# Runs selected tile by tile, halved adds and a mask made by ScalarE in a two-layer graph kernel

## The reference

```python
h = relu(layernorm(x))
W = einsum('rb,bio->rio', w_comp, weight)             # 16 types from 8 bases
x = x + segment_sum((h @ W[r])[etype, src], dst) + h_bias
h = relu(layernorm(x))
g = leaky(h @ enc_w + enc_b)                           # slope 0.1
for l in range(2):
    agg = segment_sum(g[src], dst) / max(degree, 1)
    g = leaky(agg @ lin_l_w[l] + lin_l_b[l] + g @ lin_r_w[l])
x = x + g
```

## Time and profile before

| | us |
|---|---|
| median of 3 runs | 3403.03 (3397.12 to 3404.61) |
| the profiled execution | 3396.55, its span 3394.8 |
| busy over the span | PE 2463.2 (73%), DVE 2900.7 (85%), ACT 1885.4 (56%), POOL 2461.0 (72%) |
| granted TensorE clock, mean | 0.905 |

### The profile page before, as it was taken

How to read it: one execution, slowest core, us unless ns; L and a number is a source line. 1 busy time by engine, 2 the same in 40 slices (tenths; PEclk the granted TensorE clock), 3 DMA queues, 4 the chain that set the end, 5 groups by cost and what they waited for, 6 DMA issues and landing times. The chain is left out here.

```text
span 3394.8 us, 49738 instructions
## 1 busy us (share of the span) xinstructions
PE 2463.2 (73%) x13942; PEld 1823.4 (54%) x13942; DVE 2900.7 (85%) x8116; ACT 1885.4 (56%) x4895; POOL 2461.0 (72%) x2412
## 2 busy tenths in 40 slices
PE   2999999999999588888888888657777746663000
PEld 2555555555555366666666666557777735553000
DVE  4899888888888599999999999689999978776567
ACT  1566666666666498888888888635555521110000
POOL 4477777777777477777777777577777757778871
PEclk9999999999999799999999999979999978776555
DMA  9989888887222599999999999479999989999999
GB/s 244 371 325 283 260 235 257 239 258 227 77 82 73 185 282 283 286 284 283 287 284 283 285 285 282 125 254 340 341 333 346 312 314 416 416 416 404 399 407 357
DMA packets 642447, 969.06 MB, mean 285 GB/s; under 512 B 70661, under 2 KB 412295, under 8 KB 630370
## 3 DMA queue, kind: packets, MB, share of 16 engines
q1 hardware_dynamic: 532598, 717.70, 62.9%
q0 software_dynamic: 85376, 194.22, 17.8%
q10 hardware_dynamic: 24198, 53.96, 4.7%
HBM read 509.25 MB, written 464.73 MB: 287 GB/s over the span
## 5 line engine op out<-in xcount | busy, mean ns | idle before, releaser
L972 PE MATMUL y_ps_rel<-w_basis,ht_rel 128*128 128x512 f32 x1568 | 754.3, 605 | 4.0 <-DVE two_rel L831 4.0
L709 POOL DMA_INDIRECT agg<-rows_rel,put_c x392 | 408.0, 1041 | 160.9 <-issue 96.1
L1251 ACT ACTIVATE h_node<-base_node,shift_node,rstd_node 128x128 f32<-128x128 f32 x1176 | 500.3, 483 | 1.6 <-DVE shift_node L1331 1.6
L368 POOL DMA_INDIRECT gat_rel<-in_x_dram,src_c x392 | 406.8, 1038 | 125.1 <-issue 109.9
L1111 POOL DMA_INDIRECT base_and_means<-rows_node,odd_c x392 | 388.1, 990 | 145.9 <-issue 118.0
L1102 POOL DMA_INDIRECT term_node<-agg,src_c x392 | 394.1, 1005 | 132.7 <-issue 119.6
L1792 POOL DMA_INDIRECT gat_l<-base_and_means,src_c x392 | 393.5, 1004 | 119.7 <-issue 119.4
L831 DVE SCALAR_TENSOR_TENSOR two_rel<-y_ps_rel,coef,two_rel 128x128 f32<-128x128 f32 x1568 | 438.4, 343 | 0.0
L972 PEld LDWEIGHTS y_ps_rel<-w_basis,ht_rel 128*128 128x128 f32 x1568 | 273.9, 195 | 199.2 <-issue 138.0
L984 PEld LDWEIGHTS sum_ps_rel<-same_rel,two_rel 128*128 128x128 f32 x1568 | 238.5, 192 | 191.0 <-issue 188.2
L912 ACT ACTIVATE part_rel<-y_ps_rel,coef 128x128 f32<-128x128 f32 x784 | 242.4, 361 | 159.2 <-PE y_ps_rel L972 158.7
(11 more groups left out here) (216 smaller groups left out, 6408.7 us busy)
## 6 DMA issues: line engine op xcount, KB each, us to landing
pairs_l<-base_and_means SPq DMA_DIRECT2D x112, 512.0 KB
base_and_means<-zero_row SPq DMA_DIRECT2D x49, 1024.0 KB
means<-zero_row SPq DMA_DIRECT2D x49, 1024.0 KB, 10.9
first_node<-in_x_dram SPq DMA_DIRECT2D x196, 256.0 KB, 4.1
term_node<-agg SPq DMA_DIRECT2D x196, 256.0 KB, 4.6
x<-base_node SPq DMA_DIRECT2D x196, 256.0 KB, 4.6
base_and_means<-done_node SPq DMA_DIRECT2D x196, 256.0 KB, 4.4
out_dram<-last_z_l SPq DMA_DIRECT2D x98, 512.0 KB, 10.2
```

What stands on the lines that cost most here:

```text
L368: nc.gpsimd.indirect_dma_start(gat_rel[:, m % X_RING, j, :], None, x, bass.IndirectOffsetOnAxis(ap=src_c[:, m * HALF + j:m * HALF + j + 1] ...
L709: nc.gpsimd.indirect_dma_start(agg, bass.IndirectOffsetOnAxis(ap=put_c[:, t:t + 1], axis=0), rows[:, m % KEPT, j, :], None).then_inc(s_sca ...
L972: nc.tensor.matmul(y_ps[(q + j) % 2][:, c * 512:(c + 1) * 512], ht[:, q, j, :], w_basis[:, 4 * c:4 * c + 4, :], start=True, stop=True).the ...
L1251: last = nc.scalar.activation(h[:, n % 2, j * P:(j + 1) * P], base[:, n % SLOTS, j * P:(j + 1) * P], ACT.Relu, bias=shift[:, b % 2, c:c + ...
```

## The change

AHEAD goes from 4 to 6. The spare fill of `agg` moves from SP's step 2 to step 0 and has a semaphore of its own, the one that the first scatter waits for; the spare fill of `pair` moves to step 10 (FILL_STEPS). In all stages `select` is one TENSOR_SCALAR for each tile, with the tile's column of `run_c` as a pointer scalar. In the relational stage `find_open` moves from DVE (j = 5, and the start) to ACT, as Relu(1 - run), in j = 3 ahead of the normalizing, and at the start ahead of the first deviation. The adds of the joined pass are two instructions of 256 columns. The relational stage's semaphores are cleared together with those of the joined pass, so one clear and its barrier fall away. Code of a layer 0 that isn't run is removed as well (its semaphores are no longer made).

```diff
-    AHEAD = 4
+    AHEAD = 6
...
+        waiting = []
+
         def clear(held):
 
-            nc.clear_and_free_semaphores(held)
+            nc.clear_and_free_semaphores(waiting + held)
+            waiting.clear()
             nc.all_engine_barrier()
...
                             if m == 0 and j == 0:
-                                pool.wait_ge(s_spare, 2 * DMA)
+                                pool.wait_ge(s_spare, DMA)
...
-                            if m == 2:
+                            if m == 0:
                                 sp.dma_start(agg[N:N + SPARE, :].rearrange("(p j) f -> p j f", p=P),
                                              zero_row[:].unsqueeze(1).to_broadcast([P, SPARE // P, P])).then_inc(s_spare, DMA)
+                            if m == FILL_STEPS:
                                 sp.dma_start(pair[N:N + SPARE, :].rearrange("(p j) (k f) -> p (j k) f", p=P, f=P),
-                                             zero_row[:].unsqueeze(1).to_broadcast([P, SPARE // P * 2, P])).then_inc(s_spare, DMA)
+                                             zero_row[:].unsqueeze(1).to_broadcast([P, SPARE // P * 2, P])).then_inc(s_spare_pairs, DMA)
...
                             dve.wait_ge(s_runb[q], use(m, q))
-                            nc.vector.tensor_tensor(same[:, q, :, :], columns(q),
-                                                    run_c[:, bass.ds(m * HALF, HALF)].unsqueeze(2).to_broadcast([P, HALF, P]),
-                                                    ALU.is_equal).then_inc(s_same, 1)
-
-                        def find_open(m, q):
-
-                            nc.vector.tensor_scalar(open_[:, q, :, :], columns(q), 0.0, None, ALU.is_equal).then_inc(s_open, 1)
+                            for j in range(HALF):
+                                t = m * HALF + j
+                                last = nc.vector.tensor_scalar(same[:, q, j, :], run_b[:, q, j * P:(j + 1) * P],
+                                                               run_c[:, t:t + 1], None, ALU.is_equal)
+                            last.then_inc(s_same, 1)
...
+                        def find_open(m, q):
+
+                            act.wait_ge(s_runb[q], use(m, q))
+                            nc.scalar.activation(open_[:, q, :, :], run_b[:, q, :].rearrange("p (t e) -> p t e", e=P),
+                                                 ACT.Relu, bias=ones[:, 0:1], scale=-1.0).then_inc(s_open, 1)
...
                                 ago(m, q, j, 6, keep_rows)
+                                if more and j == 3:
+                                    find_open(m + 1, 1 - q)
...
+                        find_open(0, 0)
                         deviation(0, 0)
...
-            clear(held)
+            waiting.extend(held)
...
-                            nc.vector.tensor_tensor(base[:, q, :], first[:, q, :], term[:, q, :], ALU.add).then_inc(s_base, 1)
+                            for a in range(2):
+                                part = slice(a * (BLOCK // 2), (a + 1) * (BLOCK // 2))
+                                last = nc.vector.tensor_tensor(base[:, q, part], first[:, q, part], term[:, q, part], ALU.add)
+                            last.then_inc(s_base, 1)
```

More of the change, by code:

```diff
@@ L769, in _ @@
                             sp.wait_ge(s_zeroed[k], DMA * len(range(k, 2 * FILLS, 4)))
+                        sp.wait_ge(s_spare_pairs, DMA)
                     @block.vector
@@ L865, in _ @@
                         select(0, 0)
-                        find_open(0, 0)
                         dve.wait_ge(s_border, 1)
@@ L1349, in select @@
                             dve.wait_ge(s_runb[i % 2], uses(i, 2))
-                            nc.vector.tensor_tensor(same[:, i % 2, :, :], columns(i),
-                                                    run_c[:, i * X_TILES:(i + 1) * X_TILES].unsqueeze(2)
-                                                    .to_broadcast([P, X_TILES, P]), ALU.is_equal).then_inc(s_same, 1)
+                            for j in range(X_TILES):
+                                t = i * X_TILES + j
+                                last = nc.vector.tensor_scalar(same[:, i % 2, j, :], run_b[:, i % 2, j * P:(j + 1) * P],
+                                                               run_c[:, t:t + 1], None, ALU.is_equal)
+                            last.then_inc(s_same, 1)
                         def find_open(i):
@@ L1454, in layer_pass @@
                 s_gathered = [psem(f"gathered{g}") for g in range(RING)]
-                s_added = [[psem(f"added{q}{j}") for j in range(HALF)] for q in range(2)]
                 s_runb = [psem(f"run_b{q}") for q in range(2)]
@@ L1822, in put_late @@
                                 put(rows_, edges * HALF + j, s_late[q][j])
-                        def scatter(m, j):
-                            q, t = m % 2, m * HALF + j
-                            pool.wait_ge(s_rows, tile(m, j))
-                            nc.gpsimd.indirect_dma_start(
-                                pair.rearrange("n (k f) -> (n k) f", k=2),
-                                bass.IndirectOffsetOnAxis(ap=odd_c[:, t:t + 1], axis=0), rows[:, q, j, :], None,
-                                bounds_check=2 * N - 1, oob_is_err=False).then_inc(s_added[q][j], DMA)
-                        for k in range(HALVES * HALF + LAG):
-                            if k < HALVES * HALF:
-                                gather(k // HALF, k % HALF)
-                            if k >= LAG:
-                                m, j = (k - LAG) // HALF, (k - LAG) % HALF
-                                if not l:
-                                    scatter(m, j)
-                        for q in range(2):
-                            for j in range(HALF):
-                                if not l:
-                                    pool.wait_ge(s_added[q][j], DMA * HALVES // 2)
+                        for k in range(HALVES * HALF):
+                            gather(k // HALF, k % HALF)
                         if l:
@@ L1940, in finish @@
                             act.wait_ge(s_rowed, tile(m, j))
-                            if at_least(m, 2):
-                                if not l:
-                                    act.wait_ge(s_added[q][j], use(m - 2, q))
-                                elif j == 0 and m < HALVES - KEPT:
-                                    act.wait_ge(s_spilled[q], use(m - 2, q))
+                            if m >= 2 and j == 0 and m < HALVES - KEPT:
+                                act.wait_ge(s_spilled[q], use(m - 2, q))
                             kept_at = m - (HALVES - KEPT)
```

4 lines of the change are left out of this document (1 added, 3 removed).

## The result

The changed kernel takes 3424.78 us (median of 7 runs, 3412.64 to 3432.44) against 3400.42 (7 runs, 3397.12 to 3404.61) of the kernel before on the same chip: ratio 1.007, 95% interval 1.0054 to 1.0086, slower by 0.7%. The forecast was 3414 against 3403.03.

The account below looks back on a forecast made before the run. Relational stage taken as bound by POOL's growing lag, joined pass and last layer by DVE. Terms -42 + 35 + 18 = +11 us took the median from 3403.03 to 3414; range 3370 to 3450.

Parts of the forecast that it names:

- Relational stage: First pass with its start: 53.1 us lost to POOL's lag and a late run row regained, start 8 + 3.2 later: -42 us.
- The lost 53.1 us: Relational stage, kernel before: time beyond 55 periods of 17.64 us, 6.9 for a late run row and 46 for POOL's lag.
- The fall-back of 0.67 a half: Relational stage, changed kernel: POOL loses 0.67 us a half, 34 us over 50 halves, inside its 37 us of slack.
- the 0.25 taken for blocking by small selections: Relational stage: DVE's seven small selections hold POOL up 0.25 us a half (bounds 0 and 1.1).
- Rival B: Relational stage: seven selections back to back act as one lock of 1.41 us on POOL; about 3445 us, chance 0.2.
- Rival C: Relational stage: the mask isn't covered in ScalarE, the period grows 0.3 to 0.5 us; about 3435 us, chance 0.12.
- 1.1 us a half: Relational stage, kernel before: POOL falls 1.1 us further behind PE in each half, using up its slack after 10 halves.
- Joined pass: Pass bound by DVE: selection pieces +0.16 and halved additions +0.2 us a beat, 98 beats: +35 us (bounds 0 and 45).
- it also frees POOL ... worth nothing: Joined pass: halved additions free POOL, but POOL isn't waited for there, so this was counted as worth nothing.
- Rival D: Joined pass: POOL paces the beat, so the freed 0.3 us a beat counts, -27 instead of +35; 3352 us, chance 0.08.
- Layer: Last layer, bound by DVE: seven selection pieces cost +0.33 us a half, 56 halves: +18 us (bounds 0 and 20).
- Rival E: Joined pass and layer: small pieces cost less, joined pass +12 and layer -4; 3369 us, chance 0.15.

Follow-up runs that it names:

- e10: The kernel before with only the spare fills moved (agg's to SP's step 0, pair's to step 10): 3378.24 us, ratio 0.9935.
- e1: The changed kernel with the joined pass's additions whole again (one of 512 columns): 3401.88 us, ratio 1.0014 to the kernel before.
- e2: The changed kernel with the joined pass's selection as one instruction of 512 columns again: 3410.80 us, ratio 1.0053 to the kernel before.
- e4: The changed kernel with whole additions and one selection instruction in both the joined pass and last layer: 3351.58 us, ratio 0.9862 to the kernel before.
- e9: The changed kernel with the joined pass's mask of open runs made one place earlier, ahead of g_t: 3415.88 us, ratio 1.0059 to the kernel before.
- e3: The changed kernel with the last layer's selection as one instruction of 896 columns again: 3397.81 us, ratio 1.0004 to the kernel before.
- e5: Same kernel as e9 (joined pass's mask one place earlier), run where the kernel before takes 4168 us: 4183.89 us, ratio 1.0036.
- e8: The kernel of e4 with AHEAD 4 instead of 6, run where the kernel before takes 4168 us: 4177.53 us, ratio 0.9926.
- e11: Same kernel as e8 (e4 with AHEAD 4), run where the kernel before takes 4197 us: 4158.35 us, ratio 0.9979.
- e12: The kernel of e4 with the relational selection as one instruction of 896 columns, where the kernel before takes 4197 us: 4176.75 us, ratio 1.0000.

## Why the prediction was right, and where its terms were off

The sign and the bound were right: 3424.78 measured, 3414 forecast, slower by over 0.2%. By its own steps, on the profiled executions:

**Relational stage**, forecast -42, measured -44.3. The lost 53.1 us came back whole (-53.5). The start was 9.2 us later instead of 11.2: the barrier cost 4.7 where 8 was taken from POOL's drain, and the mask ahead of the deviation 4.5 where 3.2 was taken, the difference being ScalarE's table load of 1.28 us, which the sum left out and which is no longer hidden. The fall-back of 0.67 a half was really 0.36: the 0.25 taken for blocking by small selections is zero. Rival B (a lock of 1.41 us, fourteen transfers over 18.3) is refuted by 17.94. Rival C is refuted by the period of 17.64. In the account of the kernel before, 1.1 us a half was too small by 0.17; e10 shows it. The mask and the small selections were never undone one by one where POOL binds, so how the 29 us divide between them is an estimate from lengths.

**Joined pass**, forecast +35 (0.36 a beat), measured 0.51 a beat, +48. The pieces were sized right: additions 0.21 against 0.20, selection 0.18 against 0.16. The step that failed is the sum itself: "it also frees POOL ... worth nothing". POOL's phase is worth something where DVE's tensor_scalar meets the end of a transfer. The mask then lasts 0.13 longer in nearly every beat, some 12 us in all, and it belongs to the additions' halves, since it goes with them (e1) and not with the selection (e2). Rival D (POOL paces the beat) is refuted: with POOL freed the beat is longer and POOL waits for DVE, and in e4, with stretched transfers back, it is 10.42. By the Trainium skill's page SBUF — State Buffer, section Who interferes with whom, tensor_scalar in its two-port mode and GpSimd hold a lock against each other. The forecast used it in one direction only; the table of the pieces and e9 show the other too. They don't bear out the page's "for the whole instruction": 584 of the 585 pieces that start 0.44 us or more before a transfer's end run beside it at their usual length.

**Layer**, forecast +18, measured +20 by the pieces (0.365 a half against 0.33) and some 9 that falls of the clock can account for, which the sum did not have and which differ from trace to trace. Rival E (small pieces cost less) is refuted by both stages.

Of the signs named for the forecast, the last scatter of the relational stage ended at 1089.8 (1092 named), the beat is 10.94 (10.78), two layer halves take 0.73 more (0.66).

**The size.** The sign hung on two sums against each other, -42 and +53. The gain came in within 3 us, the costs were 25 us too small, and the median's +24 is over twice the forecast's +11; that it lies well inside 3370 to 3450 is owed to the width of that range. The three costs, undone one by one, are 34, 21 and 33 us of the profiled span and 74 undone together; in medians of runs 17, 8, 21 and 67. The sum of the single medians is 21 short and that of the single spans 14 over. The spans are of one execution each, and that of the changed kernel is 5 us over its median, that of e1 6 under its own. The runs with pieces in the layer spread over 20 to 30 us (the changed kernel, e1, e2, e9), those without over 6 to 18 (e4, e3, e10, the kernel before). What spreads them is open; the falls of the clock (1.6 to 1.9 us each, a varying number) would be enough.

## What to carry to other kernels

When a producer and a consumer run at slightly different rates over a ring, work out the slack in time and the rate at which it is used up; an earlier start only puts the date off. It gave 20 us of the relational stage's 53.5, and the rest needed a shorter half of GpSimd. Splitting a VectorE instruction to free GpSimd can pay only where GpSimd is the one that is late (here some 6 us, by an estimate), and is a plain cost where VectorE bounds (some 19 and 20 us): the same edit may belong in one stage and not in the two others. Where two engines exclude each other for a few tenths and one waits for the other in each period, their phases are locked and the collision repeats in nearly every beat (94 of 98 here); look for an untouched instruction that has become longer.

## What the runs showed of the hardware

A tensor_scalar of VectorE that starts 0.2 to 0.43 us before an indirect transfer of GpSimd ends is over only after that end (at 128 columns 0.02 to 0.11 us after it, at 512 columns 0.22, with a length of 0.55 instead of 0.42); one that starts 0.44 us or more before keeps its length, but for one of 585. Seven pieces of 0.28 us, back to back, hold GpSimd up by nothing measurable, one selection of 1.08 us by 0.5 us a half.

The same kernel took a quarter longer in the sessions of e5 to e8 and of e11 and e12 than in those of e1 to e4 and of e9 and e10. The texts ahead of e9 to e12 call this another chip, which isn't shown: the record gives e1 to e4 and e11, e12 the same chip number, 1. They put it down to a low granted clock, and in the relational stage the traces do not bear that out: from 200 to 1000 us the granted clock of e12 is 0.97, matmuls and VectorE's instructions have nearly the same lengths as in e4 (its largest group of matmuls 609 ns for 593), and engines stand still with nothing in the profile to end it, as in this row of e12's waits (total, times, longest), which has no counterpart in e4:

```profile
ACT rows_rel L929 <- remote: 154.9, 61, 4.0
```

In the later stages the clock is lower as well (0.87 from 1500 to 2500 us of e12, 0.81 from 2800 to 3300), while such waits occur there too (154 us in 58 places in one row of e5's from 1500 to 2500 us); which brings on the other is not shown. What stops them is open.
